# A convolution-gated block with a top-2 mixture of experts: Pool's router piece of a step placed between its second gate multiplication and the product tt

## The reference

```python
x = x + _L0_conv_ref(_ln_c(x), conv_w, conv_b)      # norm over channels; max and mean over channels,
                                                    # 3x3 convolution, sigmoid: one gate per pixel
t = _to_tokens(x)                                   # a token is one pixel with its 64 channels
t = t + _L0_ffn_ref(_ln_t(t), router_w, router_b, expert_w, expert_b)
x = _from_tokens(t, x)

def _L0_ffn_ref(x, router_w, router_b, expert_w, expert_b):
    router_probs = jax.nn.softmax(x @ router_w + router_b, axis=-1)     # 8 experts
    top_p, top_i = jax.lax.top_k(router_probs, 2)
    top_p = top_p / jnp.sum(top_p, axis=-1, keepdims=True)
    expert_out = jnp.einsum('bnd,edc->bnec', x, expert_w) + expert_b    # 64 x 64 each
    gathered = jnp.take_along_axis(expert_out, top_i[..., None], axis=2)
    return jnp.einsum('bnk,bnkc->bnc', top_p, gathered)
```

## Time and profile before

| what | value |
|---|---|
| median of 3 runs | 1438.88 us |
| the profiled execution | 1438.13 us, its span 1436.3 us |
| busy PE, DVE, POOL, ACT | 1345.7, 1247.6, 1056.1, 1046.7 us |
| mean granted clock of TensorE | 0.974 |
| a full round (rounds 3 to 7), 14 steps | 165.1 us |

### The profile page before, as it was taken

The page is one execution under the profiler, slowest core; times in us unless marked ns, Lnnn a source line. Parts: engine busy times, 40 slices in busy tenths (PEclk is TensorE's granted clock), DMA queues, the critical chain, the costliest instruction groups (busy, mean ns, idle before and its releaser), DMA issues.

```text
span 1436.3 us, 33157 instructions
## 1 busy us (share of the span) xinstructions
PE 1345.7 (94%) x11750; PEld 632.1 (44%) x11750; DVE 1247.6 (87%) x1527; ACT 1046.7 (73%) x3949; POOL 1056.1 (74%) x659
## 2 busy tenths in 40 slices
PE   8864999999999999999999999999999998999998
PEld 8853444444444444444444444444444333333332
DVE  6786799978998889988999889998999789987776
ACT  6666888878888788888888788888888434443432
POOL 5334787787778777786777777877877887887765
PEclk9955999999999999999999999999999999999999
DMA  6442466666666666576666566566665565556563
GB/s 225 128 123 65 142 193 196 194 189 203 196 183 213 188 203 202 166 233 185 195 204 206 177 209 193 168 218 194 193 196 158 154 190 165 154 170 190 170 190 116
DMA packets 85877, 259.97 MB, mean 181 GB/s; under 512 B 13776, under 2 KB 13776, under 8 KB 85712
## 3 DMA queue, kind: packets, MB, share of 16 engines
q1 hardware_dynamic: 85712, 257.85, 59.5%
HBM read 206.42 MB, written 51.38 MB: 179 GB/s over the span
## 4 chain that ended last, share of the span: by engine, by line
PE 64%; DVE 16%; issue 8%; POOL 2%; ACT 1%; DVEq 0%; POOLq 0%; ACTq 0%
PE moe L553 37%; PE gb L499 12%; DVE gx L695 10%; PE tm L478 8%; PE tm L492 2%; PE moe L547 2%; PE tm L538 2%; DVE oh L730 2%; PE tm L577 1%; DVE ot L708 1%; DVE u L780 1%; POOL dl L1217 1%; DVE stats L672 1%; ACT gs L982 1%; POOL parts L1173 0%
## 5 line engine op out<-in xcount | busy, mean ns | idle before, releaser
L553 PE MATMUL moe<-gx,wc 128*64 128x448 f32 x3584 | 811.2, 552 | 0.0
L695 DVE TENSOR_TENSOR gx<-gb,xd 128x896 f32<-128x896 f32 x672 | 710.6, 1085 | 96.7 <-PE gb L499 93.0
L1167 POOL TENSOR_TENSOR gx<-gs,xd 128x896 f32<-128x896 f32 x224 | 477.5, 2132 | 279.2 <-ACT gs L982 148.8
L982 ACT ACTIVATE gs<-gb 128x896 f32<-128x896 f32 x224 | 205.4, 917 | 212.1 <-PE gb L499 211.8
L944 ACT ACTIVATE sq<-xct 112x64 f32<-112x64 f32 x1400 | 338.1, 244 | 7.6 <-DVE early_s L682 2.1
L553 PEld LDWEIGHTS moe<-gx,wc 128*64 128x64 f32 x3584 | 217.8, 136 | 230.5 <-issue 198.3
L499 PE MATMUL gb<-s,cg 52*128 52x448 f16 x1792 | 258.6, 356 | 43.9 <-DVE gx L695 37.2
L944 ACT ACTIVATION_READ_ACCUMULATOR sq<-xct 112x1 f32 x1400 | 263.6, 188 | 0.0
L1183 POOL TENSOR_TENSOR tt<-xc,a1s 128x896 f32<-128x896 f32 x112 | 235.9, 2107 | 11.5 <-issue 9.8
L499 PEld LDWEIGHTS gb<-s,cg 52*128 52x128 f16 x1792 | 56.9, 94 | 380.1 <-DVE gx L695 322.4
L478 PEld LDWEIGHTS tm<-rhs,xa 64*112 64x112 f32 x2800 | 171.2, 182 | 32.0 <-issue 17.8
(11 more groups left out here) (94 smaller groups left out, 1102.2 us busy)
## 6 DMA issues: line engine op xcount, KB each, us to landing
xd<-in_x_dram SPq DMA_DIRECT2D x448, 224.0 KB, 4.0
xa<-in_x_dram SPq DMA_DIRECT2D x112, 448.0 KB, 4.4
xc<-in_x_dram SPq DMA_DIRECT2D x112, 448.0 KB, 4.7
out_dram<-ot SPq DMA_DIRECT2D x112, 448.0 KB, 3.5
gx<-in_const_g_dram SPq DMA_DIRECT2D x1, 384.0 KB, 4.6
cf<-in_const_f_dram SPq DMA_DIRECT2D x1, 333.5 KB, 2.8
gx<-in_L_ffn_expert_w_dram SPq DMA_DIRECT2D x1, 128.0 KB, 4.5
cf<-in_L_ffn_expert_b_dram SPq DMA_DIRECT2D x8, 2.0 KB
```

The costliest lines, as they stand in the source:

```text
L553: last = pe.matmul(moe[b * CH:(b + 1) * CH, c, 0:HALF], wc[:, k * CH:(k + 1) * CH], gx[:, u, b, :], start=False, stop=(k == KT - 1), skip_ ...
L695: dve.tensor_tensor(gx[:, i, :, :], gb[:, 2 * slot:2 * slot + 2, 0:HALF], xd[:, v % 2, :, c * HALF:(c + 1) * HALF], ALU.mult).then_inc(sca ...
L982: act.activation(gs[:, j, :, :], gb[:, 2:4, 0:HALF], ACT.Copy).then_inc(gate_out, 1)
L1167: pool.tensor_tensor(gx[:, ND + j, :, :], gs[:, j, :, :], xd[:, v % 2, :, j * HALF:(j + 1) * HALF], ALU.mult).then_inc(scaled_p, 1)
```

## The change

Pool's two roots (`e` in step 0; `am` and `e` in step 3) get a function of their own, `router_roots`, and stay where they were, but now ahead of the tail pieces. All other router pieces of Pool move behind the second product and ahead of `tt`. `logits_scaled` of half 0 moves from step 5 to step 4, behind that step's second product. `early_body` (round 1) has the same order as before but for that step. No operation, tile or semaphore is added or removed, and PE, DVE, ACT and SP keep their orders.

```diff
             def router(r, step):
 
-                if step == 0:
-                    root_of(r, 1, stats[:, 1, :])
-                elif step == 3:
-                    affine_of_mean(r)
-                    root_of(r, 2, v2[:, :])
+                if step == 4:
+                    logits_scaled(r, 0)
                 elif step == 5:
-                    logits_scaled(r, 0)
                     logits_biased(r, 0)
...
+            def router_roots(r, step):
+
+                if step == 0:
+                    root_of(r, 1, stats[:, 1, :])
+                elif step == 3:
+                    affine_of_mean(r)
+                    root_of(r, 2, v2[:, :])
+
...
                     if parting:
                         rest_one(r, v + 2)
+                    if Bp:
+                        router_roots(r, step)
+                    if ahead:
+                        vector_place(pool, r, 2 * step + 1)
+                        scale_unit(r, v + 1, 0)
                     if tail:
                         router_tail(r - 1, step)
                     if Bp:
                         router(r, step)
                     if ahead:
-                        vector_place(pool, r, 2 * step + 1)
-                        scale_unit(r, v + 1, 0)
                         scale_x(r, v + 1)
```

## The result

| | before | with the change |
|---|---|---|
| median of 4 runs each | 1438.85 us (1438.19 to 1439.15) | 1481.24 us (1477.17 to 1483.65) |
| ratio, 95% interval | | 1.0291 [1.0278, 1.0303] |
| span of the profiled execution | 1436.3 us | 1481.9 us |
| PE's waits for DVE's `gx`, by the waits view | 37.2 us | 63.6 us |
| mean granted clock | 0.974 | 0.962 |

A forecast was written before the change was run, and what follows sets the result against it. PE, busy 94% of the span, was taken as the bound, with waits for DVE's `gx` product. Losses of 14.7 us less 5.4 us gained in round 8 made +9.3 us, named as 1448.0 us, range 1432 to 1461.

The forecast's parts named there:

- step 1, spread 2 later by: Step 1: `tt` runs from 462.96 to 465.05 and holds L788, so spread 2 comes 0.98 us late.
- step 7, spread 2 later by: Step 7: step 6's `tt` holds `key`, which ends at 536.81 in place of 535.54, a loss of 1.26 us.
- step 11, spread 2 later by: Step 11: `key` asks 0.24 us after `tt` has started and is held, 1.63 us, all a wait of PE.
- steps 8 and 12, `gap` held: Steps 8 and 12: `tt` ends 2.46 us into the step and holds `gap`; spread 2 is 0.97 us late twice.
- L730, L780 (`oh1`, `u`): Late place: `oh1` falls from 1.58 to 0.61 us (steps 7, 11); L780 freed in step 1, always 0.39 us.
- step 13, spread 2 later by: Step 13: DVE asks 0.14 us ahead of `tt` and goes first; `key` ends at 606.03, a gain of 0.23 us.
- Who asks first goes first, at the boundary of an instruction.: Two-input DVE operations and Pool instructions: the earlier asker goes first; the trace shows DVE winning when 0.17 us ahead.
- rival 2: Step 13: Pool wins too if 0.15 us earlier; `tt` holds `key`, 11.7 us more, 1459.7 us; chance 0.18.
- Round 8, "so it gets in ahead of `tt`": Round 8, without centring: pieces end about 0.35 us after DVE asks, DVE goes ahead of `tt`; net -5.4 us.
- the 9.3 us of the forecast: Whole kernel: 14.7 us lost in the full rounds and round 2, less 5.4 us in round 8, slower by 9.3.
- The forecast's last addition: Whole kernel: 1447.4 us for the profiled execution, the runs' median 0.75 higher, so 1448.0 us was named.
- how firm the two starts were: Three cases hang on 0.14 to 0.27 us between two computed starts; each is held in full or not held.

The follow-up runs named there:

- Run 4: Changed kernel with seven small added PE matmuls (`start=False`) ahead of spread 2 in steps 7, 11 and 13: 1466.07 us, ratio 1.0185.
- run 1: Changed kernel with the router pieces of steps 6, 10 and 12 back ahead of the second product: 1440.57 us, ratio 1.0010.
- run 9: Kernel before with only root `e` put ahead of tail piece `dl` in step 0: 1438.12 us, ratio 0.9991.
- run 10: Against the kernel before, Pool's pieces spread to other steps, only two behind the second product, `e` ahead of `dl`: 1426.60 us, ratio 0.9912.
- run 11: On run 10, the tail pieces one place later (`dl` in step 1, the other two in step 2): 1426.27 us, ratio 0.9911 to the kernel before.
- run 6: Changed kernel with `tt` of step 12 between L1233 and L1235: 1468.92 us, ratio 1.0205.
- run 2: Kernel before with only the pieces of steps 6, 10 and 12 moved behind the second product: 1478.55 us, ratio 1.0279.
- small (112): Changed kernel with an added 64-element Pool product on 112 partitions between L1235 and `tt` in step 12: 1459.13 us, one run.
- small (128): Changed kernel with an added 64-element Pool product on 128 partitions between L1235 and `tt` in step 12: 1481.22 us, one run.

## Why the prediction was wrong

What held, in a full round. The prediction's times are distances between spreads, so the measured ones are taken the same way: spread 2 starts 2.73 us behind spread 1 where it doesn't wait, and what is more is the wait (some 0.07 us more than the bracket of its row shows). Measured is round 5, against round 4 of the kernel before.

| place | predicted | measured |
|---|---|---|
| step 1, spread 2 later by | 0.98 us | 3.74 - 2.73 = 1.01 |
| step 7, spread 2 later by | 1.26 | 4.67 - 3.34 = 1.33 |
| step 11, spread 2 later by | 1.63 | 4.66 - 3.00 = 1.66 |
| steps 8 and 12, `gap` held | 0.97 each | 3.57 - 2.73 = 0.84 each, but 0.66 in step 12 of this round |
| L730, L780 (`oh1`, `u`) | 0.61, 0.39 | 0.61, 0.38 |
| step 13, spread 2 later by | -0.23 | 4.98 - 3.14 = 1.84 |

The mechanism of a hold was right, and rows of before gave the sizes of three of them to 0.07 us. What failed:

- **"Who asks first goes first, at the boundary of an instruction."** It fails in step 13. I had `key` 0.14 us ahead of the start of `tt` and gave it the port; it was 0.13 us ahead, and Pool went first. The starts were computed well and the rule wasn't one. It rested on `ge` ahead of L1235 alone, whose lead in the earlier trace rows is 0.13 us and not the 0.17 that the prediction names. This is rival 2, by another way than it named (Pool was no earlier). Its price of 1.95 us a round was 1.84 + 0.23 = 2.07: 12.4 us in six rounds.
- **Round 8, "so it gets in ahead of `tt`".** The same rule made a net gain of 5.4 us. The trace has DVE asking 0.39, 0.39, 0.41 and 0.73 us ahead of a `tt` and losing all four times. One of them:

```profile
1301.96 0.85 POOL L1235 TENSOR_TENSOR q<-q,rho 112x336 f32<-112x336 f32 x1
1302.05 3.29 DVE L722 TENSOR_TENSOR key<-ge,prio 112x896 bf16<-112x896 bf16 x1
...
1302.78 2.08 POOL L1183 TENSOR_TENSOR tt<-xc,a1s 128x896 f32<-128x896 f32 x1
```

PE's waits there rose from 10.2 to 13.1 us, where they should have fallen by 5.4: 8.3 us.
- **No term for TensorE's clock.** The sum made each microsecond of wait cost one microsecond. Run 4 puts 15.2 us on the clock: the wait costs itself, and some of the waits a stretch at half speed behind them.
- `gap` in the steps 8 and 12 was 0.13 us too dear each time, 1.6 us in six rounds.

Together, with the 9.3 us of the forecast: 9.3 + 12.4 + 8.3 + 15.2 - 1.6 = 43.6 us, against 42.4 measured. (The forecast's last addition, 1447.4 + 0.75, makes 1448.2 and not 1448.0.) The two profiles give a check: the span rose by 45.6 us (the profiled execution is the slowest of the four), the waits by 26.4 and PE's busy time, which half clock lengthens, by 18.0; together 44.4.

My doubt went to the wrong place. I asked how firm the two starts were, and in full rounds had seen DVE get ahead only of L1235; the step from there to `tt` was untested, and it carried two terms in one direction. That the time moved the way it was forecast owes nothing to the rule, whose two terms were both gains; it comes from the holds that were computed well.

## What to carry to other kernels

An instruction of Pool that runs over the start of a DVE operation of the shared port holds it to its own end, and moving it only moves the hold; place it by what DVE asks for in the time that it then covers, the whole chain of Pool behind it included. Where a forecast needs DVE to win a boundary by some tenths of a microsecond, price it as lost; even a row with the same two Pool instructions doesn't settle it (see below). And where a wait of PE grows towards 2 us, look at the granted clock behind it: here 26.4 us of added waits cost another 15.2 us at half clock.

## What was not expected of the hardware

**Who gets in at a boundary of two Pool instructions** doesn't follow the order in which they ask. The lead is the time from DVE's start to the start of the next Pool instruction. The table has every case in the thirteen traces in which a router operation of DVE asked while one Pool instruction ran and the next followed back to back.

| Pool's running, next | who went first | cases | lead, us |
|---|---|---|---|
| L1233, L1235 (before; runs 1, 9, 10, 11) | DVE | 35 | 0.09 to 0.82 |
| `tt`, L1235 (run 6) | DVE | 7 | 1.36 to 1.94 |
| L1173, L1226 (before; run 2) | DVE | 2 | 0.78 to 0.79 |
| L1173, L1196 (before; run 9) | DVE | 2 | 0.19 to 0.21 |
| L1173, L1196 (runs 1, 10, 11) | Pool | 3 | 0.24 to 0.42 |
| L1173, L1217 (run 1) | Pool | 1 | 0.39 |
| L1235, `tt` | Pool | 36 | 0.13 to 0.73 |
| L1217, `tt` | Pool | 16 | 0.37 to 0.41 |
| L1196, `tt` | Pool | 8 | 0.39 to 0.43 |
| L1235, the small product (112; 128) | Pool | 14 | 0.10 to 0.73 |
| small (112), `tt` | DVE | 7 | 0.40 to 1.00 |
| small (128), `tt` | Pool | 7 | 0.38 to 0.97 |

The length of the lead, the waits in front of the next instruction, the DVE operation, the partitions of the next instruction and "`tt` always wins" are each contradicted by a row. So is the pair of Pool instructions by itself: L1173 and L1196 go both ways in round 8, with the same `ge` asking. Here are the kernel before, where DVE got in, and run 10, where it didn't:

```profile
1184.03 1.21 DVE L717 TENSOR_TENSOR ge<-lg,top 112x896 bf16<-112x896 f32 x1
1184.24 2.60 POOL L1196 TENSOR_TENSOR lg<-logit_mean,rho 112x896 f32<-112x896 f32 x1
...
1173.56 2.95 DVE L717 TENSOR_TENSOR ge<-lg,top 112x896 bf16<-112x896 f32 x1
1173.82 1.75 POOL L1196 TENSOR_TENSOR lg<-logit_mean,rho 112x896 f32<-112x896 f32 x1
```

What decides stays open. One explanation that no run excludes is that the order of asking does decide, and that Pool asks for its next instruction earlier than the start that the profile shows, by a time that differs from case to case. The Trainium skill (SBUF — State Buffer, Who interferes with whom) says that issue order decides who blocks, and that agrees wherever one instruction is running; of who comes next it says nothing that would give this table.

**The end of a hold is exact.** In every case DVE ended behind the end of the Pool instruction that let it go by a constant of its operation: 0.48 us `key` and `oh`, 0.95 `ge`, 0.25 L780, L788 and L806, 0.13 to 0.14 `gap` and L775 `p`.
